# Local attention: another order of each engine's work in a tile, the second weighing a step later, q and k projected a tile further ahead, the negated maximum on ScalarE

## What is computed

```
h = shift_token(x)
q, k, v = split(h @ wqkv, 3)             # 8 heads of 64
q = l2norm(q) * qs ; k = l2norm(k) * ksc
q, k = rotary_xpos(q, k)                 # rotary with a scale that grows with the position
# windows of 128 tokens: each looks at its own and the one before, causal
sim  = einsum('bhwid,bhwjd->bhwij', q * 8, look_around(k))
sim  = where(i < j or i > j + 128 or no such token, -max, sim)
out  = einsum('bhwij,bhwjd->bhwid', softmax(sim), look_around(v))
x = x + out @ wo
```

## Time and profile before

| | us |
|---|---|
| median of 3 runs | 4295.84 |
| lowest and highest run | 4293.35, 4296.85 |
| span of the profiled execution (its only time on record) | 4300.7 |

### The profile page before, as it was taken

The page is one execution under the profiler, slowest core; times in us unless marked ns, Lnnn a source line. Parts: engine busy times, 40 slices in busy tenths (PEclk is TensorE's granted clock), DMA queues, the critical chain, the costliest instruction groups (busy, mean ns, idle before and its releaser), DMA issues. The chain is left out here.

```text
span 4300.7 us, 95101 instructions
## 1 busy us (share of the span) xinstructions
PE 3849.4 (90%) x38420; PEld 2181.8 (51%) x38420; DVE 3344.8 (78%) x5499; ACT 2570.4 (60%) x3473; POOL 1178.2 (27%) x958
## 2 busy tenths in 40 slices
PE   7999999669998969988986899999999999857996
PEld 4788888535555535555553332332333333434764
DVE  5688888769985569985787989999998978585454
ACT  3566666636654335553443777787888888635563
POOL 1122321267761067771140000000000000013552
PEclk9999999889999989999997999999999999978998
DMA  1010100133330033430062000000000000032444
GB/s 63 5 40 28 43 26 25 41 70 65 63 51 28 0 64 65 66 54 8 0 160 47 9 9 1 9 2 2 9 2 2 9 2 9 4 99 76 89 106 104
DMA packets 291062, 167.00 MB, mean 39 GB/s; under 512 B 204692, under 2 KB 281704, under 8 KB 290152
## 3 DMA queue, kind: packets, MB, share of 16 engines
q1 hardware_dynamic: 268040, 125.49, 13.4%
q0 software_dynamic: 13440, 21.24, 2.8%
q10 hardware_dynamic: 9184, 14.68, 1.0%
HBM read 77.81 MB, written 38.58 MB: 27 GB/s over the span
## 5 line engine op out<-in xcount | busy, mean ns | idle before, releaser
L2257 DVE TENSOR_REDUCE s_tops<-ps 128x2 f32<-128x1024 f32 (+3 forms) x1152 | 1251.0, 1131 | 139.9 <-PE ps L2143 101.0
L2226 ACT ACTIVATE s_weights<-ps 128x1024 f32<-128x1024 f32 (+3 forms) x1152 | 1092.6, 952 | 342.2 <-PE ps L2156 191.7
L2178 PE MATMUL ps<-s_weights,v_flat 128*32 128x256 f32 (+1 forms) x8704 | 690.8, 389 | 7.4 <-ACT s_o_t L2232 6.1
L2137 PE MATMUL ps<-keys,s_q 48*128 48x512 f16 (+3 forms) x2304 | 433.3, 373 | 46.9 <-DVE s_tops L2257 27.2
L2156 PE MATMUL ps<-s_q,keys 50*128 50x512 f16 (+3 forms) x2304 | 433.4, 373 | 46.0 <-DVE s_tops L2257 33.6
L2293 POOL CAST s_shift<-s_minus_top 128x16 f16<-128x16 f32 x32 | 6.3, 196 | 1426.8 <-DVE s_minus_top L2264 1426.8
L583 PE MATMUL ps<-a_qt,a_kt 128*128 128x256 f16 x3072 | 375.3, 273 | 3.8 <-POOL s_ones L538 3.8
L2156 PEld LDWEIGHTS ps<-s_q,keys 50*128 50x128 f16 x2304 | 112.2, 93 | 510.1 <-issue 250.1
L1174 PE MATMUL ps<-attention_w,la_yt 128*128 128x512 f16 x1152 | 290.3, 400 | 37.8 <-DMA la_yt<-la_y_parts 30.4
L583 PEld LDWEIGHTS ps<-a_qt,a_kt 128*128 128x128 f16 x3072 | 300.9, 98 | 40.3 <-POOL s_ones L538 4.2
L1249 ACT ACTIVATE la_weights<-ps 128x1024 f32<-128x1024 f32 x124 | 126.8, 1023 | 297.0 <-PE ps L1164 297.0
(11 more groups left out here) (374 smaller groups left out, 7205.5 us busy)
## 6 DMA issues: line engine op xcount, KB each, us to landing
ex_whole<-in_L_ffn_w_dram ACTq DMA_DIRECT2D x14, 1024.0 KB
qk_parts<-a_parts SPq DMA_DIRECT2D x64, 128.0 KB, 4.2
keys<-qk_parts SPq DMA_DIRECT2D x48, 128.0 KB, 5.5
s_q<-qk_parts SPq DMA_DIRECT2D x48, 128.0 KB, 4.7
x<-in_x_dram SPq DMA_DIRECT2D x8, 512.0 KB, 9.4
attention_w<-attention_split SPq DMA_DIRECT2D x2, 2048.0 KB, 9.1
la_table<-in_rotary_dram SPq DMA_DIRECT2D x64, 64.0 KB, 2.1
a_table<-in_rope_dram POOLq DMA_DIRECT2D x8, 512.0 KB, 6.3
```

The source lines that it names most:

```text
L2137: mm = pe.matmul(m.ps[:, bank, 0:width], b.q[rows(half, KEY_PARTS * L1_DH), place % 2, pair, t * P:(t + 1) * P], m.keys[rows(half, KEY_PAR ...
L2178: mm = pe.matmul(m.ps[h * QUAD:(h + 1) * QUAD, OUT, begin:end], m.v_flat[:, first:first + QUAD], weights[:, a % 2, h, begin:end], start=(k ...
L2226: act.activation(weights[:, a % 2, 2 * pair:2 * pair + 2, skip:CHUNK], m.ps[:, bank:end + 1, skip:CHUNK], ACT.Exp).then_inc(s["exp"], 1)
L2257: dve.tensor_reduce(tops[:, u % 2, :, i % 2, t, c], m.ps[:, bank:end + 1, 0:width], AX.X, ALU.max).then_inc(s["max"], 1)
```

## The change

All five `step` functions of the local attention are written in another order, and some offsets change. On TensorE `weigh(i, 1)` becomes `weigh(i - 1, 1)`, `project_o(i - 1)` becomes `project_o(i - 2)`, and `project_q`, `project_k` go from i + 4 to i + 5. `take_shift` moves from VectorE to ScalarE, as an activation with scale -1; VectorE's `find` gets a wait for it, so that `top` isn't overwritten. SyncE's queue keeps its order of DMAs, but `turn_shift`, `turn_k`, `turn_q` and `place_shift` are each one tile later in the step. On GpSimd `norms` and `normalise` of a tile stand together, and `low_o` and `low_y` come last. One more step is run at the end, and the steps of the row statistics are one later.

```diff
-    LOAD, HALF_ROWS, DOWN, ROWS, POWER, UP = 2, EARLY_TILES + 1, EARLY_TILES + 2, EARLY_TILES + 4, EARLY_TILES + 5, EARLY_TILES + 6
+    LOAD, HALF_ROWS, DOWN, ROWS, POWER, UP = 2, EARLY_TILES + 2, EARLY_TILES + 3, EARLY_TILES + 5, EARLY_TILES + 6, EARLY_TILES + 7
-            for i in range(-7, TILES + 2):
+            for i in range(-7, TILES + 3):
@@ SyncE, step(i)
                     if exists(i + 5):
                         load_table(i + 5)
+                    if exists(i + 1):
+                        turn_shift(i + 1)
                     if exists(i + 2):
-                        turn_shift(i + 2)
-                    if exists(i + 3):
-                        turn_k(i + 3)
-                        turn_q(i + 3)
-                    if exists(i + 2):
-                        place_shift(i + 2)
+                        turn_k(i + 2)
+                        turn_q(i + 2)
+                    if exists(i + 1):
+                        place_shift(i + 1)
                     if exists(i + 6):
                         turn_y(i + 6)
                     if i == LOAD:
...
@@ GpSimd, step(i)
-                    if exists(i + 3):
-                        normalise(i + 3)
                     if exists(i + 4):
                         tables(i + 4)
+                    if exists(i + 5) and i + 5 and (i + 5) % RING == 0:
+                        edge(i + 5)
+                    if exists(i + 3):
+                        add(i + 3)
+                        norms(i + 3)
+                        normalise(i + 3)
                     if exists(i - 1):
                         low_o(i - 1)
-                    if exists(i + 5) and i + 5 and (i + 5) % RING == 0:
-                        edge(i + 5)
                     if exists(i + 6):
                         low_y(i + 6)
-                    if exists(i + 4):
-                        add(i + 4)
-                        norms(i + 4)
@@ TensorE, step(i)
+                    if exists(i - 2):
+                        project_o(i - 2)
+                    if exists(i - 1):
+                        weigh(i - 1, 1)
                     if exists(i + 2):
                         find(i + 2, 0)
-                    if exists(i + 4):
-                        project_q(i + 4)
                     if exists(i):
                         score(i, 0)
-                    if exists(i + 2):
-                        find(i + 2, 1)
-                    if exists(i + 4):
-                        project_k(i + 4)
                     if exists(i + 1):
                         project_v(i + 1)
                     if exists(i):
                         score(i, 1)
+                    if exists(i + 2):
+                        find(i + 2, 1)
+                    if exists(i):
                         weigh(i, 0)
-                    if exists(i - 1):
-                        project_o(i - 1)
-                    if exists(i):
-                        weigh(i, 1)
+                    if exists(i + 5):
+                        project_q(i + 5)
+                        project_k(i + 5)
@@ ScalarE
+                def take_shift(w):
+                    act.wait_ge(s["top"], ROUNDS * (w + 1))
+                    after(act, s["shift_t"], 16 * (w - 1))
+                    act.activation(shift[:, w % 2, 0:HEADS], top[:, w % 2, :], ACT.Copy, scale=-1.0).then_inc(s["shift"], 1)
...
@@ VectorE
                 def find(w, r):
                     dve.wait_ge(s["found"], ROUNDS * w + r + 1)
                     after(dve, s["top"], ROUNDS * w + r)
+                    after(dve, s["shift"], w - 1)
...
-                def take_shift(w):
-                    dve.wait_ge(s["top"], ROUNDS * (w + 1))
-                    after(dve, s["shift_t"], 16 * (w - 1))
-                    dve.tensor_scalar(shift[:, w % 2, 0:HEADS], top[:, w % 2, :], -1.0, None, ALU.mult).then_inc(s["shift"], 1)
@@ VectorE, step(i)
                     if exists(i + 2):
-                        find(i + 2, 0)
+                        low(i + 2)
+                    if exists(i - 1):
+                        divide(i - 1, 0)
+                    if exists(i + 3):
+                        sums(i + 3)
+                    if exists(i - 3):
+                        halves(i - 3)
+                    if exists(i - 2):
+                        residual(i - 2)
                     if exists(i - 1):
                         divide(i - 1, 1)
                     if exists(i + 2):
-                        find(i + 2, 1)
-                        take_shift(i + 2)
-                    if exists(i + 3):
-                        low(i + 3)
+                        find(i + 2, 0)
                     if exists(i + 4):
                         rotate(i + 4)
-                    if exists(i):
-                        divide(i, 0)
-                    if exists(i + 4):
-                        sums(i + 4)
-                    if exists(i - 2):
-                        halves(i - 2)
-                    if exists(i - 1):
-                        residual(i - 1)
+                    if exists(i + 2):
+                        find(i + 2, 1)
```

More of the change, by code:

```diff
@@ L1290, in step @@
                 def step(i):
-                    if exists(i + 1) and i + 1:
-                        queries_for_before(i + 1)
+                    if exists(i - 1):
+                        soften(i - 1, 1)
+                    if exists(i + 4):
+                        square(i + 4)
+                    if exists(i + 7):
+                        high_y(i + 7)
+                    if exists(i + 3) and i + 3:
+                        keys_before(i + 3)
                     if exists(i):
                         soften(i, 0)
-                    if exists(i + 3):
-                        high(i + 3)
-                    if exists(i + 4):
-                        square(i + 4)
                     if exists(i - 1):
@@ L1302, in step @@
                         take_v(i + 1)
-                    if exists(i + 3) and i + 3:
-                        keys_before(i + 3)
-                    if exists(i):
-                        soften(i, 1)
-                    if exists(i + 7):
-                        high_y(i + 7)
+                    if exists(i + 3):
+                        high(i + 3)
+                    if exists(i + 2):
+                        take_shift(i + 2)
+                    if exists(i + 2) and i + 2:
+                        queries_for_before(i + 2)
                 run(step)
```

## The result

The changed kernel takes 4449.73 us (median of 4 runs, 4448.01 to 4454.28); the kernel before took 4296.35 us beside it (4293.35 to 4299.15). The ratio is 1.0351, 95% interval 1.0338 to 1.0363: 153 us slower, where +70 us was forecast. The sign and the ring were right; the size was not.

What follows compares the result with a forecast made beforehand. Before, a ring through VectorE, GpSimd and ScalarE was taken to set 12.29 us a tile; after, SyncE's queue 13.5: 26.7 + 28.8 + 12.9 + 2 = +70 us, 4366 us, range 4325 to 4408.

Steps and rivals of the forecast that it cites:

- ring A: One-tile ring through SyncE's queue: place_shift, score, soften, high_o, low_o, low_y, turn_y and back to place_shift; 13.5 us, 87%.
- The MLP's weights: SyncE's load_mlp, once a layer between turn_y and load_table, lies whole in the path: +6.4 us a layer, 12.9 together.
- the ends: First six and last five steps of each local-attention stage: +1 us a stage, between -4 and +5; +2 in all.
- I take 2.1: Landing time of a band DMA, taken from the rotary table's plain DMA; with the second issue 0.68 us later, 2.78 us.
- Rival A: The forecast itself: the ring through SyncE's queue sets the period, 13.1 to 14.3 us; own range 4343 to 4403, 87%.
- covers: VectorE's other work between sums and low, 7.4 us, hides the 6.0 us from the start of norms to low.
- rival B's ring: Ring through find, take_shift, turn_shift, turn_k, turn_q, place_shift, score, project_v, score, find sets the period: 12.55 us, 4306, 5%.
- Edits costed at nothing: TensorE's new order of the same matmuls, and take_shift on ScalarE as one ACTIVATE of some 0.3 us: no cost.
- Rival D: Waits leave TensorE idle and its clock falls to the half level in a fifth of the tiles: +70 more, 4436, 4%.
- the 0.95: Sign that the forecast is wrong: TensorE's granted clock under 0.95 in the steady part.

Runs made afterwards that it cites:

- e6_ring_a_alone: e2_add_after_low with TensorE's find(i+2,1) ahead of score(i,1): 4412.11 us, 1.0246.
- e2_add_after_low: The changed kernel with GpSimd's add made to wait until VectorE's low of the tile before is done: 4413.63 us, 1.0257.
- e5_tile_later_add_last: The changed kernel with turn_y(i+5) for turn_y(i+6) at SyncE's step end, high_y(i+7) at ScalarE's step end, and add held until low: 4364.29 us, 1.0136.
- g5_after_shift_on_vector: The changed kernel with take_shift back on VectorE, behind find(i+2,1): 4469.31 us, 1.0402.

## Why the prediction was right and wrong

**Right: ring A.** It closes as described, `turn_y` waits last for `low_y`, the shift is waited for nowhere long, `low` no longer waits for `high`. Clean, it takes 13.17 to 13.35 us in the kernels where `low` is not stretched, 13.5 forecast. The MLP's weights were right too: the round that holds them is 19.6 us in layer 0 of after and 20.3 in layer 1, some 6.4 and 7.1 above a clean ring. One sign was wrong: TensorE was to stand before the first `score` for the band's DMA, but in after it stands for q's transpose, before `find` (33.5 us in 250, against 3.7 at the band).

**The ledger.** By the starts of the scores, tiles 0 to 26 of both layers take 646.0 us before, 748.3 in `e6_ring_a_alone`, 777.7 in after (389.9 + 387.8); the last five periods 108.2, 118.1 and 129.3. The forecast's 26 x 13.5 x 2 and 12.9 for the weights make 714.9, that is +68.9, and +2 for the ends. (The prediction has 324.3 + 322.2 for before, 0.5 more, because the earlier trace rows end with the last of a score's four opening matmuls.)

- The queue's issues costed at their usual time: 748.3 less 714.9, +33 us. This is the step of the sum that failed first: "`load_table` 0.58, `turn_shift` 1.13, `turn_k` to `turn_q` 1.29, `turn_q` to `place_shift` 1.45", 4.45 us and 0.1 for handovers. In `e6_ring_a_alone` these four links take 0.80 + 1.40 + 1.40 + 1.51 = 5.11 us on the mean, because an issue now and then takes up to 2.5 us, and each such one is in the ring. The way from `score` to the exp takes 1.52 instead of 1.41, behind it 0.92 instead of 1.02.

  The step that looked weakest, "I take 2.1" for the landing, held on the mean: 2.76 us from `place_shift` to the score against 2.78, made of 2.48 in a clean round and over 3 in a late one. So the clean ring is 0.33 us shorter than my sum and the mean one 0.6 us longer. Rival A's "mean of 14.2 us" had the size, as an end and not as the value, and by late landings and not by long issues: that is luck in part. The kernel before showed the long issues already, at `turn_y` and outside the ring that bound it; I read one tile of the queue and no spread (least, median and most in ns):

```profile
L1029 SPq DMA_TRANSPOSE la_yt<-la_y_parts x20: 1213/1223/2311, 1000.1 to 1233.8; - x20
```

- VectorE's `low`, which I listed among the work that "covers" and gave 1.23 us: +29 us, after against `e6_ring_a_alone` (26 us against `e2_add_after_low`, which has the same TensorE order as after). This is the mis-sized term with the clearest cause. The `e2` pair gives 29 to 36 us for it in the whole kernel.
- The ends, +2 forecast, +21: the last five periods take 12.9 us where they took 10.8. With the add held they take 12.7, with `find` ahead of the second `score` too 11.8, so it is rival B's ring in the main. I had seen "12.6 us a period where some now take 11.5" and set it off against a lost `score`.

2 + 68.9 + 33.4 + 29.4 + 19.1 = 152.8 us, what the traces have. The ledger's terms are differences of kernels, and not each is independent of the others.

**Edits costed at nothing.** TensorE's order was not free: with the second `score` between the two `find`s, B's ring grew to 12.4 us, from some 11.4 if the estimate above holds. I priced that ring (12.55) and made it a rival, not seeing that two rings of nearly equal length both bind: with `low` stretched, opening A alone leaves the time where it was (4444.6). `take_shift` at nothing: right in the new order without the collision, wrong by some 20 us in the old; in after its move saves as much.

**Rival D** was given 4%. The clock did fall, to 0.93 and 0.94 in two windows of after, below the 0.95 I had named as the sign against me. The six stretches at the half level between 1000 and 1250 us each come in or right behind a wait of TensorE of 1.5 to 3.2 us. This is an addition to A, inside the terms above. How much of them is clock alone I didn't separate.

**Slips in the working.** Rival A's upper end has +46.9 a stage where 369.2 less 323.25 is 46.0; its +107 is right. Rival D's "busy 87%, 43 of 50" should be 84%, 42 of 50 (11.4 of 13.5 us). Neither moves the forecast.

**What bounded the kernel before.** I called `sums`, `norms`, `normalise`, `high`, `low` the ring. With `sums` first the time rises 1.0% instead of falling; with `weigh` moved it rises 2.0%. It looks as if the old order held several rings close under 12.3 us; which one sets the period stays open.

## What to carry to other kernels

Write down every one-tile ring through an in-order DMA queue, not only the longest; two of equal length hide each other in every single-edit experiment, so remove them in pairs before calling one harmless. A DMA in such a ring is to be costed at its mean, long issues and late landings included, while off the ring its usual time will do. Work that happens once and is slow to issue belongs ahead of the queue's wait and not behind it. And when two engines' instructions are moved side by side, ask whether either is slower in that company: an operation's duration from the old trace holds only beside its old neighbours.

## What the runs showed of the hardware

**VectorE's `low` and GpSimd's add don't run side by side.** `low` took 1.22 us at the least, 2.79 in the middle and 3.44 at most in layer 0 of after; held apart from the add it takes 1.22 each time (second row, `e5_tile_later_add_last`):

```profile
L1336 DVE TENSOR_TENSOR la_parts<-la_straight,la_parts x32: 1217/2788/3437, 879.1 to 1336.6; 128x1024 f16<-128x1024 f32 x32
```
```profile
L1337 DVE TENSOR_TENSOR la_parts<-la_straight,la_parts x32: 1217/1222/1248, 880.4 to 1294.2; 128x1024 f16<-128x1024 f32 x32
```

It is a block and not a slower rate: wherever the add began first, `low` takes what is left of the add and 1.1 us (2.05 us left: 3.14; 1.14 left: 2.23; 0.74 left: 1.82). In `g5_after_shift_on_vector` an operation on 8 elements comes first and takes the whole add's time, and `low` behind it is at its 1.21 us:

```profile
1102.84 2.35 POOL L1104 TENSOR_TENSOR la_straight<-la_straight,la_crossed 128x1024 f32<-128x1024 f32 x1
...
1102.86 2.36 DVE L1329 TENSOR_SCALAR la_shift<-la_top 128x8 bf16<-128x8 f32 x1
...
1105.14 1.21 DVE L1333 TENSOR_TENSOR la_parts<-la_straight,la_parts 128x1024 f16<-128x1024 f32 x1
```

It works the other way too. In the first tile of after's layer 0 `low` begins 0.16 us ahead of the add, and the add takes 3.26 us instead of 2.36:

```profile
879.10 1.22 DVE L1336 TENSOR_TENSOR la_parts<-la_straight,la_parts 128x1024 f16<-128x1024 f32 x1
879.26 3.26 POOL L1104 TENSOR_TENSOR la_straight<-la_straight,la_crossed 128x1024 f32<-128x1024 f32 x1
```

That is probably also why `take_shift` on ScalarE, where it takes 0.21 us, is the better place in after. The Trainium skill (SBUF — State Buffer, section "Who interferes with whom") says that a VectorE instruction with two SBUF inputs contends with a GpSimd instruction that reads SBUF. In the same section it says that whichever of the two issues first has the shared ports for its whole instruction, while the other blocks. The trace agrees with both: 3.43 us for `low` behind the add (1.22 + 2.36 would be 3.58), and 1.22 us for `low` ahead of it.

**Late landings and long issues come with code.** In the late round of after one packet of the instruction queue (q8) passes while q is under way; the other queue's 2144 packets take 92.3% of 5.2 us instead of 71.6% of 4.0:

```profile
q1 hardware_dynamic: 2144, 0.53, 92.3%
q8 instruction: 1, 0.02, 1.6%
...
la_qt<-la_parts SPq DMA_TRANSPOSE x1, 4.7
```
```profile
q1 hardware_dynamic: 2144, 0.53, 71.6%
...
la_qt<-la_parts SPq DMA_TRANSPOSE x1, 3.2
```

Of the 64 transposes of q in after, 23 have such an instruction packet start while they are under way: their median is 4.2 us and 18 are over 3.7. Of the 41 without one none is over 3.4. The kernel before has the same (14 of 20 against 1 of 44), but there q is in no ring that binds, and TensorE waited for it 5.1 us in 250 on its weight loads and not 38. The long issues go with the same packets: of the 320 issues of `turn_y`, `load_table`, `turn_shift`, `turn_k` and `turn_q` in after, 23 are over 0.3 us longer than usual, and each has an instruction packet start in it or in the 1 us before; of the 254 without such a packet none is long. That the code's packets make the landings late and the issues long, and don't merely come with them, no run here tested.
